# Expert tiles: the next expert's first weights converted in two pieces of 128x1408 in place of four of 128x704

## What is computed

```python
# 16 experts, each row goes to 4 of them, inner width 352
_, idx = jax.lax.top_k(masked, TOPK)
w = jnp.take_along_axis(original_scores, idx, axis=1)
...
h = jax.nn.silu(jnp.einsum('td,edh->teh', xf, w1)) * jnp.einsum('td,edh->teh', xf, w3)
y = jnp.einsum('teh,ehd,te->td', h, w2, cw)
```

## Time and profile before

| | |
|---|---|
| median of three runs | 1371.61 us (1370.1 to 1372.55) |
| the profiled execution | 1371.29 us, its span 1369.6 us |
| PE busy over the span | 1230.6 us, 90% |
| DVE, ACT, POOL busy | 53%, 40%, 31% |
| granted TensorE clock, mean | 0.954 of full speed |
| `W13` pieces on ACT (L1764) and on DVE (L1816) | 44 each |

### The profile page before, as it was taken

One profiled execution on the slowest core, in us unless ns is written; L12 is line 12 of the kernel. 1 busy time (PEld: TensorE's weight loads), 2 busy tenths in 40 slices (PEclk: granted clock), 3 DMA queues, 4 the chain that ended last, 5 costly groups with the idle time before them and its releaser, 6 DMA issues. The chain is left out here.

```text
span 1369.6 us, 25480 instructions
## 1 busy us (share of the span) xinstructions
PE 1230.6 (90%) x7821; PEld 1034.4 (76%) x7822; DVE 719.2 (53%) x1443; ACT 553.2 (40%) x1430; POOL 424.0 (31%) x504
## 2 busy tenths in 40 slices
PE   6998999999997399969998998699999989999992
PEld 6876777777776177746776876699999878999992
DVE  5666655656645589953677643442334443424340
ACT  4543444444444188833121111543344443434341
POOL 1101211211211556540005721235444433444442
PEclk9999999999998699979999999899999999999997
DMA  9000000000000111143000204555446755545456
GB/s 326 25 16 19 17 1 18 17 1 17 1 2 1 33 45 38 38 141 118 0 1 0 94 31 137 159 129 100 77 80 141 195 142 116 132 86 135 86 140 169
DMA packets 53880, 103.62 MB, mean 76 GB/s; under 512 B 5126, under 2 KB 20998, under 8 KB 53750
## 3 DMA queue, kind: packets, MB, share of 16 engines
q1 hardware_dynamic: 38182, 65.78, 14.7%
q0 software_dynamic: 15632, 36.97, 14.3%
HBM read 75.99 MB, written 30.93 MB: 78 GB/s over the span
## 5 line engine op out<-in xcount | busy, mean ns | idle before, releaser
L1738 PE MATMUL t_H<-m_W,t_xT 128*128 128x352 f32 x1632 | 286.4, 332 | 16.7 <-DVE m_W L1816 13.9
L1738 PEld LDWEIGHTS t_H<-m_W,t_xT 128*128 128x128 f32 x1632 | 268.0, 193 | 18.7 <-DVE m_W L1816 14.8
L1705 POOL DMA_INDIRECT acc_d<-t_ys,t_sid x68 | 109.2, 1606 | 279.0 <-ACT t_ys L1767 191.5
L1783 ACT ACTIVATE t_sl<-t_H 128x352 f32<-128x352 f32 x68 | 31.5, 463 | 175.4 <-PE t_H L1738 173.7
L597 ACT ACTIVATE pr<-pr 128x128 f32<-128x128 f32 x256 | 76.0, 298 | 55.2 <-DVE pr L758 53.9
L62 PE MATMUL t_Y<-m_W,t_hT 128*128 128x512 f32 (+1 forms) x207 | 88.2, 426 | 9.4 <-DVE t_hT L1861 6.4
L1837 DVE TENSOR_TENSOR t_h<-t_H,t_sl 128x352 f32<-128x352 f32 x68 | 35.5, 523 | 106.5 <-ACT t_sl L1783 106.5
L1767 ACT ACTIVATE t_ys<-t_Y,t_wcol 128x512 f32<-128x512 f32 x69 | 47.3, 685 | 94.8 <-PE t_Y L64 94.8
L1859 DVE TENSOR_TENSOR t_hT<-t_TH,t_hT 128x256 fp32r<-128x256 f32 x68 | 28.7, 422 | 107.1 <-ACT t_hT L1804 105.9
L64 PE MATMUL t_Y<-m_W,t_hT 128*128 128x512 f32 (+1 forms) x207 | 82.3, 397 | 0.0
L63 PE MATMUL t_Y<-m_W,t_hT 128*128 128x512 f32 (+1 forms) x207 | 82.0, 396 | 0.0
(11 more groups left out here) (415 smaller groups left out, 3229.6 us busy)
## 6 DMA issues: line engine op xcount, KB each, us to landing
m_r<-in_L_ffn_w_dram SPq DMA_DIRECT2D x26, 704.0 KB, 5.1
m_r<-in_L_ffn_w_dram SPq DMA_DIRECT2D x13, 512.0 KB, 3.9
aCX<-in_ctx_dram SPq DMA_DIRECT2D x20, 256.0 KB, 2.6
rows_d<-before_w SPq DMA_DIRECT2D x17, 256.0 KB, 2.0
CT<-in_ctx_dram SPq DMA_DIRECT2D x8, 512.0 KB, 3.8
X<-in_x_dram SPq DMA_DIRECT2D x4, 1024.0 KB, 13.0
acc_d<-X SPq DMA_DIRECT2D x4, 1024.0 KB, 4.2
m_r<-in_L_ffn_sw_dram SPq DMA_DIRECT2D x4, 704.0 KB, 5.4
```

The source lines that it names most:

```text
L1705: pool.indirect_dma_start(out=m["acc_d"][:, :], out_offset=bass.IndirectOffsetOnAxis(ap=sid[:, b:b + 1], axis=0), in_=ys[:, b, :], in_offs ...
L1738: x_ = pe.matmul(bk[b % 2][:, 0:I], xT[:, b % 2, jx, k, :], W13[:, jw, k, j, :], start=k == 0 and jx == jw, stop=k == KC - 1 and jx == 1)
```

## The change

ACT's copy and DVE's subtraction now take two blocks k at a time, so each has two pieces of 128x1408 for each expert. PE, which had waited before each of its four blocks, waits for the first piece before block 0 (and again, for the same count, before block 1) and for the second before block 2. All counts of the semaphores `w13_hi` and `w13_lo` go from 4 to 2 for each tile. No arithmetic, byte, buffer or transfer changes.

```diff
@@ sync
-                                sp.wait_ge(w13_lo, 4 * (n + 1))
+                                sp.wait_ge(w13_lo, 2 * (n + 1))
@@ tensor
-                                pe.wait_ge(w13_lo, 4 * n + k + 1)
+                                pe.wait_ge(w13_lo, 2 * n + k // 2 + 1)
@@ scalar
                 def w13():
-                    for k in range(KC):
-                        act.activation(W13[:, 0, k, :, :], r13[:, k, :, :], ACT.Copy).then_inc(w13_hi, 1)
+                    for k in range(0, KC, 2):
+                        act.activation(W13[:, 0, k:k + 2, :, :], r13[:, k:k + 2, :, :], ACT.Copy).then_inc(w13_hi, 1)
@@ vector
                 def w13_k(k):
-                    dve.tensor_tensor(W13[:, 1, k, :, :], r13[:, k, :, :], W13[:, 0, k, :, :].bitcast(F32), ALU.subtract)\
+                    dve.tensor_tensor(W13[:, 1, k:k + 2, :, :], r13[:, k:k + 2, :, :], W13[:, 0, k:k + 2, :, :].bitcast(F32), ALU.subtract)\
                         .then_inc(w13_lo, 1)
...
-                                for k in range(KC):
-                                    dve.wait_ge(w13_hi, 4 * (n + 1) + k + 1)
+                                for k in range(0, KC, 2):
+                                    dve.wait_ge(w13_hi, 2 * (n + 1) + k // 2 + 1)
                                     w13_k(k)
```

More of the change, by code:

```diff
@@ L1769, in _ @@
                 act.sem_inc(y_evac, 2)
-                act.sem_inc(w13_hi, KC)
+                act.sem_inc(w13_hi, KC // 2)
                 act.wait_ge(tx_fill, 1)
@@ L1823, in _ @@
                 dve.sem_inc(w2_lo, 2)
-                dve.sem_inc(w13_lo, KC)
+                dve.sem_inc(w13_lo, KC // 2)
                 dve.wait_ge(tx_hi, 1)
```

## The result

The change makes the kernel slower: 1376.53 us (1374.75 to 1379.07, 7 runs) beside 1371.61 us (1370.1 to 1373.06, 7 runs), a ratio of 1.0037 with the interval 1.0026 to 1.0048. The forecast was 1377.2 us.

What follows compares the result with a forecast made beforehand. PE, busy 90% of the span, was taken to bound the kernel. 9.45 - 3.2 - 0.9 + 0.3 = +5.65 us on 1371.29 gives 1376.9, plus 0.3 for the median: 1377.2 us, range 1374.2 to 1380.6.

Steps and rivals of the forecast that it cites:

- third term: Two pairs of one-tile experts: second pair -0.9 us if the clock stays up (+0.6 if not), first pair +0.3 us.
- First term: H stage start in seven lone conversions: first piece through ACT and DVE 1.35 us later each, +9.45 us.
- Second term: PE's seven waits for gathered rows behind conversions: they go because PE comes later, -3.2 us.
- rival 1: Stall costs more: gather waits stay (+3.2 us) or new gaps lower clock (+1.5 us each); 1379 to 1382 us; 9%.
- +0.64 us for `W2`'s transfer: Second pair: DVE's subtraction for `W2` starts 0.64 us later, which sets the raw second weights' transfer and PE's last wait.
- two clock terms: Second pair, clock staying up after 2.1 us idle: -1.08 us to the next H stage, -0.44 us in that stage.
- rival 2: PE hardly waits, stall lies within gather waits: no tellable change, 1371 to 1373 us; 10% with cases up to forecast.
- rival 3: Faster: y evacuation leaves ACT 0.16 us sooner and gathers come sooner by that, 1369 us; 3%.
- Rival 1's clock: New gaps of 1.35 + 0.10 us before H stage bring clock down, +1.5 us each; rival 1 in all 9%.

Runs made afterwards that it cites:

- three-piece split: Kernel before with pieces of 704, 704 and 1408 elements on both ACT and DVE; 1373.36 us, ratio 1.0013.
- held-back scatter: Kernel with only ACT in two pieces, plus POOL waiting before each scatter until DVE's subtractions are through; 1374.05 us, ratio 1.0029.
- hi products first: Kernel before with PE doing the 16 products that need only W13 hi before the 8 that need W13 lo; 1371.79 us, ratio 0.9998.

## Why the prediction was right

The stall and the waits that it swallows were right in mechanism and size. That the time came within 0.7 us of the forecast is luck besides: in the profile the third term is 1.8 us lower than forecast, and 1.7 us that the sum didn't have make up for it.

- **First term: right.** 1.32 us a conversion for 1.35 forecast, the copy 1.366 us for 1.38, the subtraction 1.622 for 1.63. Undoing either half and the three-piece split put it on the first piece's way, and on what covers the others.
- **Second term: right in size (-3.0 for -3.2), one step wrong.** "The scatter starts some 0.16 us sooner" holds (4.02 us after the first copy, 4.21 before), but not what should follow: its issue took 2.02 us, so the gather was issued 6.35 us after the copy where it had been 6.13, and where the trace has its landing, that was 13.2 to 13.5 us after the copy, before 12.6 to 13.1. The 1.32 us covered it, as the text had allowed for. Its argument against rival 1, that gather and scatter start before the transfer does, misread the trace: in the kernel before the gather was issued at 1060.61, behind the weights:

```profile
1058.84 0.95 SPq L990 DMA_DIRECT2D m_r<-in_L_ffn_w_dram  x2
```

  By the held-back scatter the landing goes with the start of those weights (4.81 us after the copy in the change, before 4.36) and not with the gather's issue. Where the stall was smaller (ACT alone, 0.59 us, weights after 4.94) the later landing made me miss by 3 us.
- **Third term: mis-sized, -2.4 in place of -0.6 us.** The clock stayed up as forecast (1.00 in 1136 to 1138, before 0.50), but not since the idle time fell to 2.1 us: there was none. The part of the sum that failed is the +0.64 us for `W2`'s transfer, which let it take as long as before: counted from tile 34's H stage, PE's first matmul with `W2` came 0.72 us sooner (35.55 us, before 36.27). The two clock terms came as forecast: 2.43 us in place of 3.51 to the next H stage, and 0.49 us less for the tile behind. In the changed kernel ACT's copy of `W2` waited for no transfer:

```profile
1126.83 0.40 SPq L996 DMA_DIRECT2D m_r<-in_L_ffn_w_dram  x1
...
1132.76 1.05 ACT L1797 ACTIVATE m_W<-m_r 128x1024 fp32r<-128x1024 f32 x1
1133.67 1.60 POOL L1705 DMA_INDIRECT acc_d<-t_ys,t_sid  x1 [6.17 <-ACT t_ys L1767]
```

  So it landed within 5.9 us; before it took 7.46 us,

```profile
1122.98 0.40 SPq L996 DMA_DIRECT2D m_r<-in_L_ffn_w_dram  x1
```

  and a scatter was issued into it 4.8 us after its start, where now it comes after 6.8. The other traces bear out only part of that reason. In the four versions with hi products first the scatter came 4.1 to 4.7 us after the start of this transfer and ACT's copy, waiting for it, 5.9 to 6.4; in four others the scatter came after 5.3 to 6.4 and the copy after 5.2 to 5.7; but with DVE alone in two pieces the scatter came after 6.2 and the copy after 6.8. None has 7.5 us again, and the kernel before was profiled once, so how much of the -2.4 us comes in every execution stays open. Tile 36 spent longer at the low clock (9.31 us in place of 8.46), which the wait of the kernel before would have swallowed.

  That the clock stays up after 2.1 us idle was not put to the test here, and length alone doesn't decide it: it fell after 2.26 and 2.48 us in the first pairs of two versions with hi products first, and stayed at 1.00 after 2.47 us in the kernel before.
- **Missing: +1.1 us at trip ends and +0.7 behind the last tile.** Behind tile 63 PE stood 0.57 us for nothing that the trace shows. From the transposes to the H stage it is 0.61 to 1.06 us there in all four profiles with DVE in two pieces of 1408, and 0.25 to 0.29 in those of the kernel before and of the others, that with one piece too. The cause stays open.
- **Rivals.** A stall within the gather waits (rival 2) and an earlier evacuation that wins (rival 3) did not occur; the second is what ACT alone in two pieces tests, with a loss. Rival 1's clock does not come at 1.18 us idle, and does at 3.88. Its other half, gather waits that stay, did not occur in the change and did with ACT alone in two pieces.

## What to carry to other kernels

Join pieces only where the one that waits has cover for the first long one, and count what follows the last: a transfer that it releases and an engine that it holds up. A wait that the change makes longer upstream may swallow one that stands downstream, so list the small waits of the next tiles before summing. And where a gather needs nothing of the scatter in front of it, issue it first: that was worth more (-0.45%, under half of it in the stretches of the lone conversions) than any choice of pieces.

## What the runs showed of the hardware

A scatter's issue on POOL took 1.60 to 1.61 us in 67 of the 68 cases of the kernel before, and 1.65 in one. Where it started while DVE was still in the subtraction of `W13`, whose operands both lie in the on-chip memory (SBUF), it ended 1.47 to 1.49 us after the end of that subtraction (1.51 to 1.53 in the first pair), whatever the start: 2.02 us in the change, 2.15 with ACT alone in two, 3.28 with one piece:

```profile
1073.27 3.09 DVE L1815 TENSOR_TENSOR m_W<-m_r,m_W 128x2816 fp32r<-128x2816 f32 x1 [1.81 <-ACT m_W L1763]
1074.56 3.28 POOL L1705 DMA_INDIRECT acc_d<-t_ys,t_sid  x1 [4.35 <-ACT t_ys L1766]
```

1074.56 + 3.28 - 1073.27 - 3.09 = 1.48; in the change 1060.04 + 2.02 - 1057.42 - 3.16 = 1.48. Held back until DVE was through with `W13`, it took 1.61, and 1.80 where it met the subtraction of `W2`, 1.48 us past whose end it ended as well. Beside DVE's work on matmul results in PSUM, the banks that PE writes (L1859), it was 1.60 as well.

It works one way only. Where the scatter started first, such a subtraction hardly lengthened it: in the two pairs of the kernel before, the subtraction of `W2` started 0.14 and 0.17 us behind the scatter, and the scatter took 1.65 and 1.61 us. The second is

```profile
1120.27 1.61 POOL L1705 DMA_INDIRECT acc_d<-t_ys,t_sid  x1 [9.90 <-ACT t_ys L1767]
```

with the subtraction from 1120.43, which takes its usual 1.23 us. And a subtraction right behind the first one doesn't hold the scatter on: in the second pair of the change `W2`'s follow `W13`'s without a gap and run on beside the scatter, which still ended 1.48 us after the end of `W13`'s.

The Trainium skill, "SBUF — State Buffer", section "SBUF: two separate sides", says that a DVE instruction with two SBUF inputs and a GpSimd one that reads SBUF exclude each other on the port pair that they share, and that whichever starts first has it for the whole instruction. The traces agree where DVE starts first (2.02, 2.15 and 3.28 us) and not where POOL's issue does (1.61 us, with a subtraction of 1.23 us that starts and ends inside it, as long as ever). I had not looked for it when I let the scatter come sooner.
